# Output product of self-attention in seven stationary tiles for four heads, with packed low parts

## What is computed

```python
Wdkv = x @ latent_w + latent_b                                # 72 latents per token
q = jnp.einsum('btc,hcl->bhtl', x, Wd_w) + Wd_b[None, :, None, :]   # 16 heads
scores = jnp.einsum('bhtl,bsl->bhts', q, Wdkv) / jnp.asarray(np.sqrt(d_head), dtype=x.dtype)
scores = jnp.where(causal[None, None, :, :], scores, -jnp.inf)
attn = jax.nn.softmax(scores, axis=-1)
y = jnp.einsum('bhts,bsl->bhtl', attn, Wdkv)
z = jnp.transpose(y, (0, 2, 1, 3)).reshape(b, t, h * Wdkv.shape[-1])
return z @ out_w + out_b                                      # 16 x 72 -> 256
```

## Time and profile before

| | |
|---|---|
| median of 3 runs | 3108.91 us (3107.84 to 3109.11) |
| the profiled execution | 3108.85 us |
| its span | 3106.2 us |
| self-attention | about 0 to 1175 us of the span |
| cross-attention, then experts | 1175 to 3106 us |

### The profile page before, as it was taken

One profiled execution on the slowest core, in us unless ns is written; L12 is line 12 of the kernel. 1 busy time (PEld: TensorE's weight loads), 2 busy tenths in 40 slices (PEclk: granted clock), 3 DMA queues, 4 the chain that ended last, 5 costly groups with the idle time before them and its releaser, 6 DMA issues. The chain is left out here.

```text
span 3106.2 us, 72903 instructions
## 1 busy us (share of the span) xinstructions
PE 3080.1 (99%) x22657; PEld 2893.5 (93%) x22657; DVE 2258.3 (73%) x6587; ACT 2144.2 (69%) x6949; POOL 1594.6 (51%) x2918
## 2 busy tenths in 40 slices
PE   9999999999999999999999999999999999999998
PEld 7999999999999999999999999999988888889998
DVE  7888888877777877778878787787865555454665
ACT  8888888888888887878777787887744444442222
POOL 5677677666676665333333333333456666652000
PEclk9999999999999999999999999999999999999999
DMA  5455555444444460211111211111355445433333
GB/s 165 126 149 156 149 153 153 137 120 125 124 113 113 127 213 29 65 45 49 62 46 49 65 46 49 62 45 49 103 135 110 102 103 115 113 54 91 126 122 102
DMA packets 202274, 315.29 MB, mean 102 GB/s; under 512 B 34753, under 2 KB 135745, under 8 KB 200929
## 3 DMA queue, kind: packets, MB, share of 16 engines
q1 hardware_dynamic: 177376, 277.82, 29.7%
q0 software_dynamic: 24576, 33.57, 6.4%
HBM read 125.20 MB, written 75.50 MB: 65 GB/s over the span
## 5 line engine op out<-in xcount | busy, mean ns | idle before, releaser
L1141 POOL TENSOR_SCALAR ca_prob<-ca_prob,ca_inverse 128x120 f32<-128x120 f32 x1024 | 355.2, 366 | 615.4 <-DVE ca_inverse L1440 613.4
L824 ACT ACTIVATE sa_prob<-sa_prob,sa_shift 128x128 f32<-128x128 f32 (+1 forms) x1024 | 453.9, 462 | 0.0
L1381 ACT ACTIVATE ca_prob<-bank,ca_shift 128x120 f32<-128x120 f32 x1024 | 353.9, 366 | 1.8 <-DVE ca_shift L1434 0.6
L879 DVE CUSTOM_DVE_ANT_0 sa_prob<-bank,sa_mask 128x128 f32<-128x128 f32 (+1 forms) x1024 | 304.4, 352 | 0.9 <-issue 0.2
L570 POOL TENSOR_SCALAR sa_prob<-sa_prob,sa_inverse 128x128 f32<-128x128 f32 x512 | 198.4, 387 | 199.1 <-DVE sa_inverse L891 190.5
L137 PE MATMUL bank<-sa_ow,sa_y_hi 128*128 128x256 f32 x1024 | 278.1, 303 | 0.0
L139 PE MATMUL bank<-sa_kvT_b,sa_q 112*128 112x128 f32 (+1 forms) x1024 | 260.6, 280 | 0.0
L920 DVE TENSOR_TENSOR sa_pT_lo<-bank,sa_pT_hi 128x384 fp32r<-128x384 f32 x512 | 257.8, 543 | 0.2 <-ACT sa_pT_hi L811 0.2
L139 PE MATMUL bank<-sa_ow,sa_y_lo 112*128 112x256 f32 x1024 | 257.6, 282 | 0.0
L137 PE MATMUL bank<-sa_kvT_a,sa_q 128*128 128x128 f32 (+1 forms) x1024 | 248.9, 279 | 1.0 <-DVE sa_shift L879 0.8
L572 POOL TENSOR_SCALAR sa_prob<-sa_prob,sa_inverse 128x256 f32<-128x256 f32 x512 | 246.4, 481 | 0.0
(11 more groups left out here) (274 smaller groups left out, 12036.4 us busy)
## 6 DMA issues: line engine op xcount, KB each, us to landing
sa_q<-sa_q_tile SPq DMA_DIRECT2D x125, 288.0 KB
sa_q<-sa_q_tile SPq DMA_DIRECT2D x157, 112.0 KB
mid_x2T<-ca_x2T SPq DMA_DIRECT2D x32, 512.0 KB
ex_sx<-mid_x2T SPq DMA_DIRECT2D x32, 512.0 KB
sa_q<-sa_q_tile SPq DMA_DIRECT2D x297, 32.0 KB
sa_xT_raw<-in_xT SPq DMA_DIRECT2D x32, 256.0 KB, 2.9
sa_q<-sa_q_tile SPq DMA_DIRECT2D x32, 256.0 KB
sa_x_res<-in_x SPq DMA_DIRECT2D x32, 256.0 KB
```

What stands on the lines that cost most here:

```text
L824: act.activation(prob[:, r, hh, cols], prob[:, r, hh, cols], ACT.Exp, bias=shift[:, r, n:n + 1], scale=-1.0, accum_out=total[:, r, n:n + 1 ...
L879: dve.tensor_tensor_reduce(out=prob[:, r, hh, cols], in0=SC[hh][:, t * T:t * T + (t + 1) * P], in1=mask[:].rearrange("p a s -> p (a s)")[: ...
L1141: ins = pool.tensor_scalar(prob[:, r, t, hh], prob[:, r, t, hh], inverse[:, r, n:n + 1], 1.0, ALU.mult, ALU.mult)
L1381: act.activation(prob[:, r, t, hh], SC[g % 2][:, n * S:n * S + S], ACT.Exp, bias=shift[:, r, n:n + 1], accum_out=total[:, r, n:n + 1]).the ...
```

## The change

Four heads (a quad: two pairs, for both rows of a group four steps) share three low tiles. The low rows of the quad's first head are cut in three pieces of 24 rows and moved into the free rows 72 to 95 of the other three heads' tiles, and its 16 repeated high rows into rows 112 to 127 of the third head's. The weight tiles `ow_b` are laid out to match. Four transfers on the SP queue do that for both rows of the group at once, behind the q moves of the slot in which the second step of the quad had its PV; `y_in` counts them. The first pair of a quad then runs only its high tiles in its slot; its second head's low tile runs two slots later, with the second pair. `y_lo` gets a ring of 6 instead of 4, `x_res` is loaded in slots 4 and 5 of the next group, and the split of the output weights takes two DVE operations.

```diff
@@ -176,6 +176,9 @@
 DIRECT = 6
 OW_RING = 3
 SA_BODY = 32
+QUAD = 4
+Y_RING = 6
+GAP = AT - L
 SA_BODIES = B * NP // SA_BODY
 SA_GROUPS = SA_BODY // (2 * NP)
 GROUP = 2 * NP
...
@@ -200,6 +203,16 @@
 def upto_tile(J, t, per=1, more=0):
 
     return J * (SA_GROUPS * QT * per) + (per * (t + 1) + more)
+
+
+def upto_quad(J, g, per=1):
+
+    return J * (SA_BODY // QUAD * per) + per * (g // QUAD + 1)
+
+
+def y_at(J, g):
+
+    return (SA_BODY * J + g) % Y_RING
 
 
 def slot_exists(J, g):
...
-    y_hi, y_lo = al.split("y", [P, RING, 2, T])
+    y_hi, y_lo = al.sb("y_hi", [P, RING, 2, T], F32R), al.sb("y_lo", [P, Y_RING, 2, T], F32R)
...
-    RES_IN, RES = (13, 14), (GROUP + 6, GROUP + 9)
+    RES_IN, RES = (GROUP + 4, GROUP + 5), (GROUP + 6, GROUP + 9)
...
+            g = m - PL
+            if slot_exists(J, g) and g % QUAD == 1:
+                y, n, r = y_at(J, g - 1), y_at(J, g + 1), (g - 1) % RING
+                need_alone(sp, ylo_done, upto_slot(J, g), spare_sp)
+                need(sp, o_mm, upto_slot(J, g - 2))
+                for to, rows, frm in ((y_lo[L:AT, y:y + 2, 1], slice(0, GAP), y_lo), (y_lo[L:AT, n:n + 2, 0], slice(GAP, 2 * GAP), y_lo),
+                                      (y_lo[P - REST:P, n:n + 2, 0], slice(0, REST), y_hi), (y_lo[L:AT, n:n + 2, 1], slice(2 * GAP, L), y_lo)):
+                    at = r if frm is y_hi else y
+                    sp.dma_start(f32(to), f32(frm[rows, at:at + 2, 0])).then_inc(y_in, 16)
             if u == X_NEXT and group_exists(J, c + 1):
                 need(sp, xlo_done, upto_row(J, c, 1))
                 load_xT(J, c + 1)

...
             for c, i in due(J, m, RES_IN):
                 need(sp, o_read, upto_row(J, c, i - 2))
+                if isinstance(J, int) and J * SA_GROUPS + c == 0:
+                    sp.wait_ge(ow_done, 2 * (2 * OW_RING))
                 sp.dma_start(x_res[:, i], d["x"][J * (2 * SA_GROUPS) + (2 * c + i)].rearrange("(t p) c -> p t c", p=P)).then_inc(res_in[i], 16)
...
-                pool.tensor_scalar(y_lo[AT:AT + REST, r], f32(y_hi[0:REST, r]), 1.0, 1.0, ALU.mult, ALU.mult).then_inc(ydup_done, 1)
+                own = slice(int(g % QUAD < 2), 2)
+                pool.tensor_scalar(y_lo[AT:AT + REST, y_at(J, g), own], f32(y_hi[0:REST, r, own]), 1.0, 1.0, ALU.mult, ALU.mult).then_inc(ydup_done, 1)
...
@@ -727,16 +752,23 @@
                 need(pe, ylo_done, upto_slot(J, g))
                 need(pe, ydup_done, upto_slot(J, g))
                 if first_body(J) and c == 0 and i == 0:
-                    pe.wait_ge(ow_done, p + 1)
+                    pe.wait_ge(ow_done, 2 * (p + 1))
                 if p == 0:
                     need(pe, o_read, upto_row(J, c, i - 2))
-                for hh in range(2):
+                y = y_at(J, g)
+                parts = [(y_hi, r, 0, 0), (y_hi, r, 0, 1)]
+                if p % 2 == 1:
+                    parts += [(y_lo, y_at(J, g - 2), 1, -1), (y_lo, y, 1, 0), (y_lo, y, 1, 1)]
+                for part, n, a, hh in parts:
+                    if a == 1 and hh < 0:
+                        need(pe, y_in, upto_quad(J, g, 64))
                     w = slice((2 * p + hh) * C, (2 * p + hh + 1) * C)
+                    rows = slice(0, AT + REST if a == 1 and hh != 0 else P)
                     for t in range(TT):
                         tk = slice(t * P, t * P + P)
-
-                        mm = two(pe, O[i][:, t * C:t * C + C], y_hi[:, r, hh, tk], y_lo[:, r, hh, tk], ow[:, 0, w],
-                                 ow[:, 1, w], p == 0 and hh == 0 and t == 0, p == NP - 1 and hh == 1)
+                        mm = pe.matmul(O[i][:, t * C:t * C + C], part[rows, n, hh % 2, tk], ow[rows, a, w],
+                                       start=p == 0 and a == 0 and hh == 0 and t == 0, stop=p == NP - 1 and a == 1 and hh == 1,
+                                       skip_group_check=True)
                 mm.then_inc(o_mm, 1)
 
         return slot
...
                 need(act, o_mm, upto_slot(J, g - RING))
+                if g % QUAD < 2:
+                    need(act, y_in, upto_quad(J, g - QUAD, 64))
                 act.activation(y_hi[:, r].rearrange("l h t -> l (h t)"), PV[:], ACT.Copy).then_inc(yhi_done, 1)
             g = m - TL
             if slot_exists(J, g):

...
             dve.wait_ge(owhi_done, p + 1)
-            dve.scalar_tensor_tensor(out=part, in0=f32(part), scalar=minus_low[:, 0:1], in1=raw,
-                                     op0=ALU.mult, op1=ALU.add).then_inc(ow_done, 1)
+            for a in range(2):
+                cols = slice(C if a == 1 and p % 2 == 0 else 0, 2 * C)
+                dve.scalar_tensor_tensor(out=part[:, a, cols], in0=f32(part[:, a, cols]), scalar=minus_low[:, a:a + 1], in1=raw[:, a, cols],
+                                         op0=ALU.mult, op1=ALU.add).then_inc(ow_done, 1)
...
                 need(dve, yhi_done, upto_slot(J, g))
-                dve.tensor_tensor(y_lo[0:AT, r].rearrange("l h t -> l (h t)"), PV[0:AT, :],
-                                  f32(y_hi[0:AT, r].rearrange("l h t -> l (h t)")), ALU.subtract).then_inc(ylo_done, 1)
+                dve.tensor_tensor(y_lo[0:L, y_at(J, g)].rearrange("l h t -> l (h t)"), PV[0:L, :],
+                                  f32(y_hi[0:L, r].rearrange("l h t -> l (h t)")), ALU.subtract).then_inc(ylo_done, 1)
...
@@ -2329,6 +2365,17 @@
         return np.concatenate((v, np.take(v, range(REST, L), axis)), axis)
 
     ow = a("L0_attn_out_w").reshape(H, L, C).transpose(1, 0, 2).reshape(L, H * C)
+
+    def filled(h):
+
+        own, lent, n = ow[:, h * C:(h + 1) * C], ow[:, (h - h % QUAD) * C:(h - h % QUAD + 1) * C], h % QUAD
+        rows = np.zeros((P, C), ow.dtype)
+        if n > 0:
+            rows[:L], rows[L:AT], rows[AT:AT + REST] = own, lent[(n - 1) * GAP:n * GAP], own[:REST]
+        if n == 2:
+            rows[AT + REST:] = lent[:REST]
+        return rows
+
     laid = {
         "x": a("x"), "xT": t("x"), "ctxT": t("ctx_1024"),
         "wd": a("L0_attn_Wd_w").transpose(1, 0, 2).reshape(C, H * L),
...
-        "ow_b": np.concatenate((ow, np.zeros((AT - L, H * C), ow.dtype), ow[:REST], np.zeros((P - AT - REST, H * C), ow.dtype))),
+        "ow_b": np.concatenate([filled(h) for h in range(H)], 1),
```

More of the change, by code:

```diff
@@ L283, in self_attention @@
     qbias, lbias, hbias = al.sb("qbias", [P, QT]), al.sb("lbias", [P, 1]), al.sb("hbias", [P, DIRECT])
-    minus_low = al.sb("minus_low", [P, 1])
+    minus_low = al.sb("minus_low", [P, 2])
     mask = al.sb("mask", [P, 3, P])
@@ L296, in self_attention @@
         used = KC * (H * L + P + DIRECT * P)
-        first.enter_context(nc.sbuf_tensor("sa_below", [P, 4 * RING * T + 2 * TT * C - used], F32))
+        first.enter_context(nc.sbuf_tensor("sa_below", [P, 2 * (RING + Y_RING) * T - used], F32))
         ow_raw = first.enter_context(nc.sbuf_tensor("sa_ow_raw", [P, OW_RING, 2, 2 * C], F32))
@@ L300, in self_attention @@
     pT_hi, pT_lo = al.split("pT", [P, 2, 2, 3 * P])
-    y_hi, y_lo = al.split("y", [P, RING, 2, T])
-    x_res = al.sb("x_res", [P, 2, TT, C])
+    y_hi, y_lo = al.sb("y_hi", [P, RING, 2, T], F32R), al.sb("y_lo", [P, Y_RING, 2, T], F32R)
     res = al.sb("res", [P, 2, TT, C])
     x1 = al.sb("x1", [P, 2, TT, C])
-    al.sb("behind", [P, 2 * H * C - 4 * RING * T - 3 * 2 * TT * C])
+    x_res = al.sb("x_res", [P, 2, TT, C])
     obias, half = al.sb("obias", [P, C]), al.sb("half", [P, TT])
@@ L343, in self_attention @@
     ydup_done = al.sem("ydup_done")
+    y_in = al.sem("y_in")
     q_mm, qhi_done, qlo_done = al.sem("q_mm"), al.sem("qhi_done"), al.sem("qlo_done")
@@ L376, in self_attention @@
     STAGE_FROM, STAGE_STEP = 40, 6
-    sthi_done, stlo_done = Later(owhi_done, NP), Later(ow_done, NP)
+    sthi_done, stlo_done = Later(owhi_done, NP), Later(ow_done, 2 * NP)
     WV_IN, WK_IN, WQ_HI_IN, WQ_LO_IN, WO_IN = 0, 1, 2, 4, 6
@@ L522, in slot @@
                     if m == at:
-                        sp.wait_ge(ow_done, p - OW_RING + 1)
+                        sp.wait_ge(ow_done, 2 * (p - OW_RING + 1))
                         load_ow(p)
@@ L545, in gpsimd @@
         pool.affine_select(out=minus_low[:], in_=minus_low[:], compare_op=ALU.is_ge, fill=0.0, base=-L,
-                           pattern=[[0, 1]], channel_multiplier=1).then_inc(const, 1)
+                           pattern=[[-GAP, 2]], channel_multiplier=1).then_inc(const, 1)
         pool.affine_select(out=mask[:, 0], in_=mask[:, 0], compare_op=ALU.is_ge, fill=MASKED, base=0,
```

## The result

The changed kernel takes 3128.4 us (median of 5 runs, 3123.2 to 3131.2) against 3108.9 before: ratio 1.0063, interval 1.0052 to 1.0074. It is slower by 0.6%, where 0.6% faster was forecast. The profiled execution took 3128.81 us with a span of 3126.3.

What follows compares the result with a forecast made beforehand. TensorE, busy back to back, was taken as the bound. The terms -30.7 + 7.2 + 1 + 3.8 + 1 gave -17.7 us, so 3108.9 would become 3091 us, with a range of 3080 to 3105, 8 in 10.

Steps and rivals of the forecast that it cites:

- Matmuls removed: Self-attention output product on TensorE: 256 fewer matmuls at 0.12 us each, -30.7 us gross.
- Slot 1 and `kv_lo`: TensorE's wait for `kv_lo` absorbs slot 1's 0.48 us in 15 groups: 7.2 us given back, plus 1 us for weight staging.
- The other short slots: Other even slots: ACT, the nearest chain, has idle time that fits the removed 0.48 us; cost 0.
- Rival B: Uneven slots: ACT or DVE holds the even slots while odd ones still pay, making it slower, 3140 us; chance 0.04.
- The SP queue: Packing sets of 2.9 us delay q moves for slot 8's scores: 1.5 us plus 2.3 us, 3.8 us; bounds 0 to 13.
- Rival C: SP queue binds: at 4.5 us a set, slot 8 waits 1.6 us more in 15 groups, 3115 us; chance 0.14.
- the 4 us point: SP cost per packing set from which the queue decides; put at 3105 us, the upper end of the range.
- New waits: TensorE in odd slots, ACT before `y_hi` and SP itself: sets land in time, cost 0.
- The end: Self-attention's last slots: 1 us given back by two short slots; last sets beside 8 MB of weights, 0 to 3, taken as 0.
- Rival D: Sets land late: TensorE in odd slots or ACT before `y_hi` waits 1 us in 64 quads, 3108 to 3155; chance 0.03.

Runs made afterwards that it cites:

- Run 1: Changed kernel with the packing transfers, and TensorE's and ScalarE's waits for them, left out after the first three quads: 3092.0 us, ratio 0.9951.
- run 9: Changed kernel with packing transfers cut to an eighth of their columns after the first three quads, same number and order: 3126.5 us, ratio 1.0058.
- run 10: Changed kernel with the 24-partition packing transfers cut to 16 partitions after the first three quads: 3116.6 us, ratio 1.0031.
- The order edit: Changed kernel's xT loads moved to slot 1 and x_res loads to slots 0 and 1 on the SP queue; alone it measured 3112.2 us.
- run 3: Changed kernel with xT loads moved from slot 3 to 1 and x_res loads from slots 4 and 5 to 0 and 1: 3112.2 us, ratio 1.0017.
- run 6: Changed kernel with xT and x_res loads moved earlier (first group's x_res kept in place) and slot 2's q tile behind PV: 3099.2 us, ratio 0.9964.
- run 11: Run 6's kernel plus cross-attention weights issued behind packing transfers, staging every eight slots, last two output-weight loads in slots 16 and 17: 3085.4 us, ratio 0.9927.
- the last kernel: The kernel of run 11, changed kernel with reordered loads, q tile, cross-attention weights and staging: 3085.4 us, ratio 0.9927.

## Why the prediction was wrong, point by point

**Matmuls removed, -30.7 us: right.** 28.1 us in 14 groups and 3.2 in the others. Even slots without a q tile take 3.11 us, as the text said. The 27.9 us by the gap that the Trainium skill (TensorE: Matmul & The Clock Gate, Back-to-back issue gap) gives for an isolated matmul would have been further off.

**Slot 1 and `kv_lo`, +8.2 us: right.** Slots 1 and 2 lose 12.4 us for 3.2, 9.2 more in 14 groups. The q tile of slot 2 waits 0.72 us for 0.23, against 0.71 forecast.

**The other short slots, 0: right.** Run 1 shows nothing there. Rival B falls.

**The SP queue, 3.8 us: wrong, 33 us.** This is the step that failed: the term of 0.1 us for each of 15 groups and 2.3 us for staging and output weights came out as 26.5 us at slot 8 and 6.7 in slots 9 to 15. The place and the mechanism were right; the sizes were not. In the late group shown, the forecast had the q moves of slot 5 end 2.1 us later against the scores of slot 8; they end 3.1 us later. The set takes 3.26 us (889.79 to 893.05), not 2.9: it was priced from the 24-row q moves, which read one run of each partition, while a packing transfer reads and writes two, 0.81 us for 0.72. The larger part is the eight q moves themselves, 6.31 us from first to last, where the earlier trace rows shows 5.55; one of them took 1.28 us. I had taken one clean group as the rule. In the kernel before, the same eight took 5.53 to 6.47 us in the 15 groups, 5.84 in the mean, and that could have been read ahead. Moves of 1 us or more number 23 of 913 between 80 and 1120 us before, where none shows in the time of slots 7 to 15, and 42 of 897 after. From the end of the last issue to the first matmul it takes 1.44 us at the least, not 1.2 + 0.16 = 1.36. Together that is 1.1 us past a slack of 0.4. After 620 us five of seven groups wait 0.3 to 1.2 us at slot 8, where 0.1 was forecast for each.

In the groups with staging or output-weight loads the q moves also land later behind those loads (up to 2.7 and 4.1 us from the last issue to the first matmul, for 1.44). There waits of 2 us and more came, four of them, and behind three of the four the lower clock, a cost that stood in no term: 6.7 us of the 26.5, by coincidence the same figure as that of slots 9 to 15.

Rival C named this, "if one set cost 4.5 us", and put the point where it decides at 4 us. It decides at 3.25, because the slack that it was measured against was that of a clean group. The range of 0 to 13 us for the term ended below what came: it bounded the set alone, not the set together with irregular moves. Its upper end took 1.08 us as the largest issue from a row that shows two issues together. And by the rival's own steps (24 us at 4.5 us a set, 9 at 3.5) the 4 us point is 3107.7 us, not the 3105 at which the range ends. Against rival C the text held that "the issue time follows the partition count"; the earlier trace rows already has a 32-row move at 0.55 us beside the 24-row one at 0.72 (see below on the hardware).

The DMA page of the Trainium skill (DMA: Bandwidth & Descriptors, Issuing engines are not separate DMA queues) calls the sequencer's time usually small beside the DMA. That does not hold for the small transfers of this queue: 0.81 us to issue stands against about 1.4 us to land, and in the groups an eighth of the bytes changed nothing (run 9), shorter issues did (run 10). The text also called the queue one "that hardly pauses"; it waited for q tiles for 249 us of 1050.

**New waits, 0: nearly right in the groups, wrong at the end.** TensorE waits for a packing transfer by 0.3 us in the groups. The 6.7 us of slots 9 to 15 go when the sets go (run 1), so they are the sets' doing. The order edit took them to 2.1 us in run 3 but left 3.8 in run 6 and 5.5 in run 11, so that they are the queue's backlog in other places is shown in part only.

**The end, 1 us with 0 to 3 for the weights: wrong, 7.3 us.** "By my count they land in time by under 1 us" counted issues. The set of slot 3 was issued by 1168.8 and landed at about 1178, behind five weight transfers of a megabyte each. Rival D has its place here, once and not in 64 quads. The 3.93 us wait took the clock with it.

## What to carry to other kernels

Before transfers are added to a queue, read what the queue itself waits for over the whole stage: it had 249 us of idle time in 1050, and 64 sets of 3.25 us take 208. The total alone does not decide, though: the last kernel's queue waits for q tiles for 60 us, less than the changed kernel's 83, and TensorE hardly waits for it. What decides is whether the idle time lies between the added transfers and the next one that something waits for. A slack read in one clean period is an upper bound; the periods with staging, and the one long issue in twenty, decide. A queue that is full hides other gains: the same reordering of TensorE gave 3.6 us before the change and nothing on it, and once the x loads had been moved to slots in which the queue was idle it kept 3.9 of its 10.6 us in the groups.

## What the runs showed of the hardware

An issue on SP of these small transfers has its price neither by bytes nor in proportion to its partitions, but mainly by whether their number is a multiple of 16. The q moves of the kernel before come in many sizes (80 to 1120 us; median issue time of each in us; one run of 2 or 4 KB per partition):

| partitions | 16 | 32 | 48 | 64 | 8 | 24 | 40 | 56 | 72 |
|---|---|---|---|---|---|---|---|---|---|
| 4 KB | 0.59 | 0.56 | 0.57 | 0.53 | 0.67 | 0.75 | 0.74 | 0.78 | 0.79 |
| 2 KB | 0.56 | 0.59 | 0.59 | | 0.64 | 0.72 | 0.73 | 0.78 | |

So 64 partitions of 4 KB issue faster than 24 of 2 KB. A second run per partition adds up to 0.1 us (0.81 for 24 partitions at 1 KB and at 128 B a run, 0.59 to 0.66 for 16). Run 10's step from 24 to 16 partitions is the same one. The Trainium skill (DMA: Bandwidth & Descriptors, Why a DMA increments its semaphore by 16 and not by 1) says that a transfer uses the largest number of engines up to 16 that divides its partitions, by which 24 would use 12 and 16 all. The trace agrees: the semaphore of a packing set gets 55 updates in each of the 64 sets, which is 12 and one more for each of the three 24-partition transfers and 16 for the other, and 64 with 16 partitions each (run 10). Why the issue takes longer then, no run here separates. A set cut so that its transfers have 16, 32 or 48 partitions would be worth trying.

After a long stop TensorE can come back at half clock. Behind the wait of 2.06 us at 172.72 the windows show 0.62 and 0.53 of full speed for some 3.5 us, that is 1.2 GHz for 2.4; behind the 3.93 us wait 0.50 for 6 us. Behind 1.26 us at 616.04 it stayed at 1.00, and also behind 2.31 us at 247.35, while behind 2.30 us at 395.31 it fell to 0.58 and 0.56 in the two windows from 396 on. So the length of the stop alone does not settle it; what does is open. One such dip costs 1.65 us (slot 8 behind 172.72; 1.63 behind 395.31), nearly as much as the wait that brought it.

```profile
174.00:176.00 2.00, 2.00 (x7) 1.61 (x6) 0.89 (x7) 0.10 (x1) 1.07 (x4) 0.62 0.92 234
176.00:178.00 2.00, 2.00 (x9) 1.72 (x8) 0.75 (x1) 0.77 (x2) 0.70 (x2) 0.53 0.37 80
...
248.00:250.00 2.00, 2.00 (x13) 1.70 (x12) 1.29 (x9) 0.06 (x1) 0.29 (x1) 1.00 1.01 345
...
396.00:398.00 2.00, 2.00 (x10) 1.62 (x9) 1.29 (x9) 0.00 (x0) 1.24 (x4) 0.58 1.03 291
398.00:400.00 2.00, 2.00 (x7) 1.57 (x6) 0.20 (x1) 0.69 (x1) 1.29 (x4) 0.56 0.79 227
```

Left open: why single q moves take 1 to 2.2 us to issue, and what holds 5.5 us in slots 9 to 15 of the last kernel.
